# Batch 0's output projection, normalisation and router logits moved into the last attention unit, its shared feed-forward moved ahead of batch 1's projection

## The chip, the cores and the metric

One core of one Trainium2 chip runs the whole layer in one launch. The metric is the device time of that launch in microseconds (us); for the kernel before it is 554.7 us, the median of three runs (551.94, 554.70 and 554.82).

## What is computed

Two post-normalised blocks on 2048 tokens (B = 2 batches of T = 1024) of width 256, all in float32:

```python
x = _layernorm(x + attn(x, Wq, Wk, Wv, Wo))   # 16 heads of 16, 4 key/value heads, ALiBi, causal softmax
...
logits = x @ router_w.T                       # 8 experts, the best one per token
scores = sigmoid(top_vals)                    # of the chosen expert alone
routed = (up * silu(gate)) @ down_proj[e]     # on x * score, by expert
shared = silu(x @ shared_gate_w) * (x @ shared_up_w) @ shared_down_w
x = _layernorm(x + shared + routed)
```

The norms have no weights. The shared feed-forward (hidden width 512) is done for every token; the routed one for the one expert of each token.

## The kernel before, in words

Each engine has its own program, written out by hand, and the engines meet at semaphores only. An engine runs its program strictly in the order of the code, so a wait holds up all that stands behind it. The same is true of SP, which issues nearly all DMAs, and of POOL, which issues the rest.

**Attention.** The work is cut into NU = 8 units, one for each batch and key/value head (four query heads); units 0 to 3 are batch 0, units 4 to 7 are batch 1. A unit is 9 groups of four tiles. A tile is one score matmul of 128 keys by 512 queries (`score`, L528, matmul at L537), one exp on ACT into `probs` (`weights`, L802, at L807) and two 32-column float32 matmuls with the values (`weigh`, L540, at L548). Scores go through SB = 3 PSUM banks (4, 5, 6), so the score of tile i waits for the exp of tile i - 3. POOL zeroes half of the diagonal tiles (L1155). `step(u)` on PE (L564) walks the nine groups by the strings in `ORDER`: S is a score, W the weighing of the group before, M a row-maximum tile of the next units (`max_tile`, L506), which DVE reduces (L879). In the last unit no M is left: its groups hold SSSWS alone. The maxima of unit 7 are taken during unit 6; DVE then turns them (L913 to L930) and SP writes them back (`max_rows`, L317). ACT copies the two banks of outputs and denominators to SBUF, one in the middle of the unit and one after its end (L816, L821), and SP stores them to DRAM as `yT` (`store_y`, L311).

**Between attention and experts.** For each batch SP loads the denominators from DRAM (`load_den`, L327), DVE inverts them (`invert`, L943), SP stores the result and waits until it is there (`store_rden`, L332), and loads it in another layout (`load_rden`, L346); the unnormalised outputs come with 8 DMAs per chunk of 512 tokens (`load_yT`, L338). For batch 0 all this happens while unit 7 runs (L433 to L438), for batch 1 after it (L440 to L450). There are NCH = 4 chunks, 0 and 1 of batch 0. PE does for each chunk c `spread(c)` (L605, one reciprocal to all rows, two instructions of 512 columns), `project(c)` (L612, four token tiles, two matmuls, so four instructions of 256 columns, each, in banks 2 and 3 by turns) and `route(c)` (L624: eight transposes, a copy of them by ACT at L830, and 16 logit instructions of 8 columns). DVE does `normalise(c)` (L949), `residual(c)` (L954: an add, a bn_stats and a bn_aggr for each tile) and `scale_rows(c)` (L965), with the inverse root on POOL between them (L1173). The order on PE is L672 to L703, on DVE L971 to L982. After the fourth chunk one pass chooses the expert of all 2048 tokens (L996 to L1008), PE ranks the tokens (L694 to L701), and DVE works out each token's slot (L1023 to L1045).

**Shared feed-forward.** `gate_up(n)` (L642) for n = 0 to 15: chunk n // 4, hidden block n % 4, eight instructions of 512 columns; it waits for `hidden(n - 2)`. ACT does Silu (L837), DVE the product (`hidden`, L1010). `down(c)` (L652) is 32 instructions of 256 columns; DVE adds the result into `x_all` (L1056). That add also waits until POOL has scaled the tile's rows by the score (L1189), since it overwrites them. POOL then scatters the rows by expert with 16 indirect DMAs (L1193). PE's order is `gate_up(0)`, `route(3)`, `gate_up(1)`, the ranking, then L702 to L715.

**Experts.** 23 tiles of 128 rows (L756 to L762). The change only swaps the PSUM banks of their gate and up products.

Where the buffers lie: `x1T` (the turned, normalised tokens) is in `probs`, which the last unit is using until its end; `hT` and `sG` of the shared feed-forward are in `tmp`, beside `yTc`, `rdc` and `den`.

Of the kernel before, what the change touches and what calls it, by code (L numbers as in the profile page):

```python
# [11 lines left out]
P = 128  # L12
# [88 lines left out]
ORDER = (SHORT, LONG) * 4 + (SHORT,)  # L101
assert NA % 2 == 0 and GROUPS % STEP == 0 and sum(o.count("M") for o in ORDER) == NA

# [18 lines left out]
def layer(nc, x_d, xT_d, wq_d, wk_d, wv_d, wo_d, rt_d, gu_d, dn_d, sg_d, su_d, sd_d, cf_d, cb_d, al_d, one_d, zero_d, thq_d, thk_d,  # L122
          out_d):
    with ExitStack() as ctx:
# [33 lines left out]
        x1T = pr2[:, 0:KC * NTOK].rearrange("p (k t) -> p k t", k=KC)  # L158
# [22 lines left out]
        hT = tmp[:, 0:2048].rearrange("p (f t) -> p f t", f=FC)  # L181
        hT0 = tmp[:, 3072:3584]
        sG = [tmp[:, 2048 + i * 512:2048 + (i + 1) * 512] for i in range(2)]
# [42 lines left out]
        def hidden_part(c, f):  # L226

            return hT0 if f == 0 and c % 2 else hT[:, f, :]

# [54 lines left out]
        def _(sp):  # L284
# [194 lines left out]
        def _(pe):  # L479
# [121 lines left out]
            for u in range(NU):  # L601
                step(u)


            def spread(c):  # L605

                pe.wait_ge(s_ch[c], 16 * (KC * TPC + 1))
                if c >= 2:
                    pe.wait_ge(s_yn, c - 1)
                pe.matmul(ps[:, c % 2, :], sel, rdc[c % 2], start=True, stop=True).then_inc(s_rb, 1)  # L610

            def project(c):  # L612
                pe.wait_ge(s_yn, c + 1)
                for t in range(TPC):
                    n = c * TPC + t
                    at = TPC - 1 - t if c % 2 else t
                    if n >= 2:
                        pe.wait_ge(s_res, n - 1)
                    for kc in range(KC):
                        mm = pe.matmul(ps[:, 2 + n % 2, 0:C], yTc[c % 3][:, kc, at * P:(at + 1) * P], wo[:, kc, :],  # L620
                                       start=kc == 0, stop=kc == KC - 1)
                    mm.then_inc(s_op, 1)

            def route(c):  # L624
# [3 lines left out]
                for kc in range(KC):  # L628
                    for t in range(TPC):
                        mm = pe.transpose(ps[:, 4 + kc, t * P:(t + 1) * P],  # L630
                                          x_all[:, c * TPC + t, kc * P:(kc + 1) * P], idf)
                    mm.then_inc(s_tp, 1)
                pe.wait_ge(s_x1T, KC * (c + 1))
                for t in range(TPC):
                    n = c * TPC + t
                    for kc in range(KC):
                        mm = pe.matmul(ps[:, 6, n * E:(n + 1) * E], x1T[:, kc, n * P:(n + 1) * P], rt[:, kc, :],  # L637
                                       start=kc == 0, stop=kc == KC - 1)
                mm.then_inc(s_lg, 1)


            def gate_up(n):  # L642
                c, f = n // FC, n % FC
                if n >= 2:
                    pe.wait_ge(s_h, n - 1)
                for w, bank, done in ((wsg, 0, s_g), (wsu, 1, s_u)):
                    for kc in range(KC):
                        mm = pe.matmul(ps[:, bank + 2 * (n % 2), :], w[:, kc, f * P:(f + 1) * P],  # L648
                                       x1T[:, kc, c * CH:(c + 1) * CH], start=kc == 0, stop=kc == KC - 1)
                    mm.then_inc(done, 1)  # L650

            def down(c):  # L652
                pe.wait_ge(s_h, FC * (c + 1))
                for t in range(TPC):
                    n = c * TPC + t
                    if n >= 2:
                        pe.wait_ge(s_acc, n - 1)
                    for f in range(FC):
                        mm = pe.matmul(ps[:, 4 + n % 2, 0:H], hidden_part(c, f)[:, t * P:(t + 1) * P], wsd[:, f, :],  # L659
# [12 lines left out]
            pe.wait_ge(s_wo, 32)  # L672
            pe.wait_ge(s_yev, 2 * NU + 2)
            spread(0)
            for c in range(NCH):
                if c % 2 == 0:
                    spread(c + 1)
                project(c)
                if c >= 1:
                    route(c - 1)  # L680
# [605 lines left out]
```

## Time and profile before

| what | us |
|---|---|
| median of three runs | 554.70 |
| the profiled execution's own time | 557.83 |
| its span, first to last instruction | 556.1 |
| PE busy in the span | 514.5 (93%) |
| DVE busy | 298.9 (54%) |
| ACT busy | 229.1 (41%) |
| POOL busy | 177.5 (32%) |
| mean granted TensorE clock, as a share of 2.4 GHz | 0.972 |

The profile is of one execution. PE, DVE, ACT and POOL are the compute engines, PEld is PE's weight load, which runs beside its matmuls, SP issues DMAs (SPq is its queue). "Busy" is time in which an instruction is under way; the granted clock says at which of TensorE's two speeds (1.0 is 2.4 GHz, 0.50 is 1.2 GHz). Matmuls overlap, so the spacing of their starts, and not the duration of one, says what a row of them costs. L with a number is a line of the kernel before. PE's share of the chain that ended last is 81%.

### The profile page before, as it was taken

Reading aid. Unit: us, or ns where it says so; the run is one execution under the profiler, and the core shown is the slowest. Engines: PE = TensorE matmul, PEld = TensorE weight load, DVE = VectorE, ACT = ScalarE, POOL = GpSimd, SP = SyncE. Lnnn points to the kernel's source line nnn. Section 1 sums busy time; section 2 is a strip of 40 time slices with the busy share of each in tenths; the row PEclk is TensorE's granted clock in tenths of the full one; section 3 lists DMA queues with packets and bytes.
Section 4 is the critical chain, followed back from the end, with each engine's and each line's share of the span. In section 5 each row is a group of like instructions: output and inputs, shape, how many; then the busy total and the mean of one; then the engine's idle time right before and its main releaser. Section 6 shows DMA issues by size and latency. Waiting matters only on the chain.

```text
span 556.1 us, 7466 instructions
## 1 busy us (share of the span) xinstructions
PE 514.5 (93%) x2538; PEld 256.4 (46%) x2538; DVE 298.9 (54%) x624; ACT 229.1 (41%) x465; POOL 177.5 (32%) x247
## 2 busy tenths in 40 slices
PE   5987999999999999988889899989999999999991
PEld 2432333333333333321166655555656666566661
DVE  1789888888888888860075451211213333334241
ACT  3441676767676767678601131101112222322220
POOL 4432223322222222222100109730022554545543
PEclk9999999999999999999977989999999999999997
DMA  7772455545453545071328100320121221222210
GB/s 225 134 194 73 78 170 89 159 89 175 86 180 87 179 82 183 20 239 47 101 66 285 44 0 1 132 76 20 57 85 49 66 76 59 68 76 57 66 48 28
DMA packets 36868, 54.92 MB, mean 99 GB/s; under 512 B 5647, under 2 KB 24931, under 8 KB 36724
## 3 DMA queue, kind: packets, MB, share of 16 engines
q1 hardware_dynamic: 29792, 30.96, 21.3%
q0 software_dynamic: 7040, 23.50, 13.5%
q8 instruction: 21, 0.34, 0.3%
q14 instruction: 15, 0.12, 0.1%
HBM read 34.76 MB, written 17.52 MB: 94 GB/s over the span
## 4 chain that ended last, share of the span: by engine, by line
PE 81%; DVE 10%; ACT 4%; issue 2%; DMA 1%; POOL 1%; POOLq 0%; SPq 0%; ACTq 0%; DVEq 0%
PE ps L728 14%; PE ps L548 11%; PE ps L523 10%; PE ps L648 10%; PE ps L537 9%; DVE mx L879 7%; PE ps L747 7%; PE ps L659 5%; PE ps L493 3%; PE ps L620 3%; PE ps L739 2%; ACT probs L807 2%; PE ps L525 2%; PE ps L637 1%; PE ps L610 1%
## 5 line engine op out<-in xcount | busy, mean ns | idle before, releaser
L879 DVE TENSOR_REDUCE mx<-ps 128x1 f32<-128x512 f32 (+4 forms) x312 | 183.0, 643 | 29.0 <-PE ps L525 20.9
L807 ACT ACTIVATE probs<-ps 128x512 f32<-128x512 f32 x288 | 151.1, 606 | 68.6 <-PE ps L537 68.6
L523 PE MATMUL ps<-qk_or_dn 127*128 127x512 bf16 (+3 forms) x384 | 117.4, 331 | 5.5 <-DVE mx L879 3.9
L537 PE MATMUL ps<-qk_or_dn 127*128 127x512 bf16 x288 | 100.5, 380 | 2.9 <-ACT probs L807 2.6
L1155 POOL TENSOR_SCALAR_AFFINE_SELECT probs<-probs 128x512 f32<-128x512 f32 x64 | 40.5, 633 | 164.5 <-ACT probs L807 164.5
L728 PE MATMUL ps<-wgu,tmp 128*128 x184 | 82.9, 593 | 0.1
L548 PE MATMUL ps<-probs,Vs 128*32 128x512 f32 x576 | 76.7, 605 | 0.7 <-ACT probs L807 0.7
L523 PEld LDWEIGHTS ps<-qk_or_dn 127*128 127x128 bf16 x384 | 37.1, 97 | 80.1 <-DVE mx L879 63.7
L1203 POOL DMA_INDIRECT rows<-acc,tok x23 | 22.7, 986 | 89.9 <-DMA acc<-x_all 45.1
L1068 DVE TENSOR_TENSOR tmp<-tmp,ps 128x512 f32<-128x512 f32 x23 | 15.8, 688 | 65.0 <-PE ps L728 65.0
L525 PE MATMUL ps<-cb 128*128 128x128 bf16 x256 | 50.6, 222 | 0.0
L728 PEld LDWEIGHTS ps<-wgu,tmp 128*128 128x128 f32 x184 | 33.3, 190 | 33.3 <-issue 33.3
L537 PEld LDWEIGHTS ps<-qk_or_dn 127*128 127x128 bf16 x288 | 27.1, 98 | 41.7 <-ACT probs L807 23.6
L860 ACT ACTIVATE tmp<-ps 128x512 f32<-128x512 f32 x23 | 13.7, 597 | 74.9 <-PE ps L739 74.9
L747 PE MATMUL ps<-qk_or_dn,tmp 128*128 x184 | 43.6, 380 | 0.8 <-ACT tmp L860 0.8
L747 PEld LDWEIGHTS ps<-qk_or_dn,tmp 128*128 128x128 f32 x184 | 34.9, 190 | 15.1 <-issue 11.5
L837 ACT ACTIVATE tmp<-ps 128x512 f32<-128x512 f32 x16 | 9.4, 597 | 65.2 <-PE ps L648 59.5
L525 PEld LDWEIGHTS ps<-cb 128*128 128x128 bf16 x256 | 25.1, 98 | 14.1 <-issue 1.3
L648 PE MATMUL ps<-probs,wsu 128*128 128x512 f32 x64 | 31.2, 611 | 0.0
L659 PE MATMUL ps<-wsd,tmp 128*128 128x256 f32 x128 | 28.8, 381 | 2.3 <-issue 1.4
L648 PE MATMUL ps<-probs,wsg 128*128 128x512 f32 x64 | 30.9, 606 | 0.0
L493 PE MATMUL ps<-probs,yU 128*128 128x512 f32 x48 | 24.4, 645 | 6.0 <-DMA yU<-in_wq 6.0
(121 smaller groups left out, 470.9 us busy)
## 6 DMA issues: line engine op xcount, KB each, us to landing
wgu<-in_gu POOLq DMA_DIRECT2D x8, 1024.0 KB, 6.1
qk_or_dn<-qparts SPq DMA_DIRECT2D x36, 128.0 KB
yT<-yU SPq DMA_DIRECT2D x16, 256.0 KB, 2.1
qk_or_dn<-in_dn SPq DMA_DIRECT2D x8, 512.0 KB, 8.0
tmp<-xs SPq DMA_DIRECT2D x23, 128.5 KB
qparts<-wgu SPq DMA_DIRECT2D x6, 384.0 KB, 3.3
tmp<-yT SPq DMA_DIRECT2D x34, 64.0 KB
xs<-rows POOLq DMA_DIRECT2D x1, 2056.0 KB, 10.2
```

The costliest lines, as they stand in the source:

```text
L493: mm = pe.matmul(ps[:, 4 + n % 4, :], w, xTc[:, c, kc, :], start=kc == 0, stop=kc == KC - 1)
L523: mm = pe.matmul(o, q, K6[k][0:KROWS, k0:k0 + w], start=True, stop=not masked)
L525: mm = pe.matmul(o[:, diag:diag + P], id16, mask_qk, start=False, stop=True)
L537: pe.matmul(o, K6[k][0:KROWS, kb * P:(kb + 1) * P], Q6[k][0:KROWS, :, qi * P:(qi + 1) * P], start=True, stop=True).then_inc(s_st, 1)
L548: mm = pe.matmul(ps[32 * j:32 * j + VP, 2 + bank, :], Vs[:, u % STEP, kb, :], probs[:, 4 * (s % 3) + p, :], start=begins, stop=ends, skip_ ...
L648: mm = pe.matmul(ps[:, bank + 2 * (n % 2), :], w[:, kc, f * P:(f + 1) * P], x1T[:, kc, c * CH:(c + 1) * CH], start=kc == 0, stop=kc == KC - 1)
L659: mm = pe.matmul(ps[:, 4 + n % 2, 0:H], hidden_part(c, f)[:, t * P:(t + 1) * P], wsd[:, f, :], start=f == 0, stop=f == FC - 1)
L728: mm = pe.matmul(ps[:, 2 * k + half_i, :], xsT[k][:, kc, :], wgu[:, bass.ds(e * (KC * 2 * I) + (kc * 2 * I + half_i * I), I)], start=kc == ...
L747: mm = pe.matmul(ps[:, 7, 0:H], ehT[j % 2][:, f, :], wdn[:, bass.ds(experts[j] * (FC * H) + f * H, H)], start=f == 0, stop=f == FC - 1)
L807: act.activation(probs[:, 4 * (s % 3) + p, :], ps[:, 4 + (4 * s + p) % SB, :], ACT.Exp, scale=SCALE).then_inc(s_exp, 1)
L879: dve.tensor_reduce(o, ps[:, a_bank(u, t), 0:nh * w].rearrange("p (h w) -> p h w", h=nh), AX.X, ALU.max).then_inc(s_amax, 1)
L1155: pool.affine_select(tile, tile, [[0, HG], [1, P]], ALU.is_ge, zero, base=0, channel_multiplier=-1).then_inc(s_mask, 1)
```

## The change

- In the last unit PE follows `LAST_ORDER` in place of `ORDER`: in group 3 both spreads of batch 0 (R), in groups 4 and 5 the eight projections of its tiles (P), in group 7 the transposes of chunk 0 (T), in group 8 its logits (L). DVE, ACT and POOL get the matching work at the matching places of their programs.
- SP loads batch 0's denominators and its 16 pieces of `yT` before its step of unit 6, no longer after it. `store_rden(0)` and the two `load_rden` stay after that step. `invert(0)` moves into DVE's stream of maxima for unit 7, eight tiles from its end.
- `route` is split into `turn` (transposes) and `logits`. After the last unit PE does the four `gate_up` of chunk 0 with chunk 1's transposes and logits between them, then spreads and projects batch 1, then `down(0)`, then chunk 1's `gate_up` with the transposes, logits and ranking of batch 1 between them.
- The choice of the expert is done for each batch by itself (`choose`, `confidence`, `odds`), so ACT's Exp at the old L832 comes twice, between Silus. POOL scales batch 0's rows before it does the inverse roots of chunks 2 and 3.
- `x1T` of batch 0 moves to the part of `qk_or_dn` that no longer holds a unit; the down-projection weights of experts 4 and 5, which go there, are loaded last, after `gate_up(7)`. `hT` and `sG` move to `probs`. PSUM banks are dealt out anew.

```diff
+LAST_ORDER = ("SSSWS", "SSSWS", "SRSSWRS", "SPSPSPWPS", "SPSPSPWPS", "SSSWS", "STSSWS", "SLSSWS", "W")
...
+        x1T = [qk_or_dn[:, 2 * KC * T:3 * KC * T].rearrange("p (k t) -> p k t", k=KC),
+               pr2[:, 0:KC * T].rearrange("p (k t) -> p k t", k=KC)]
...
             for u in range(NU):
+                if u == NU - 2:
+                    load_den(0)
+                    for c in range(2):
+                        load_yT(c)
                 step(u, u % STEP, last=u == NU - 1, more=u + 2 < NU)
                 if u == NU - 2:
-                    load_den(0)
                     store_rden(0)
                     for c in range(2):
-                        load_yT(c)
                         load_rden(c)
...
             for c in range(2, NCH):
-                if c == 3:
-                    sp.wait_ge(s_op, TPC)
-                    load_yT(c)
                 sp.wait_ge(s_rb, c - 1)
                 load_rden(c)
-            for e in range(E):
+                if c == 2:
+                    sp.wait_ge(s_op, TPC)
+                    load_yT(3)
+            for e in (0, 1, 2, 3, 6, 7, 4, 5):
+                if e == 4:
+                    sp.wait_ge(s_u, 2 * FC)
...
             pe.wait_ge(s_wsh, 48)
             gate_up(0)
+            turn(1)
             gate_up(1)
+            logits(1)
             gate_up(2)
             gate_up(3)
-            for c in range(NCH):
+            spread(2)
+            spread(3)
+            for n in range(NT // 2, NT):
+                project(n)
+            down(0)
+            turn(2)
+            gate_up(4)
+            turn(3)
+            gate_up(5)
+            logits(2)
+            logits(3)
+            gate_up(6)
+            rank()
+            gate_up(7)
+            for c in range(1, NCH):
...
                 for s in range(1, GROUPS):
                     weights(u, s)
+                    if last and s == GROUPS - 2:
+                        copy_turned(0)
...
+                if n == 4:
+                    copy_turned(2)
+                if n == 5:
+                    copy_turned(3)
+                act.activation(sG[n % 2], ps[:, gate_bank(n), :], ACT.Silu).then_inc(s_sg, 1)
+                if n == 0:
+                    copy_turned(1)
+                if n in (1, 5):
+                    odds(n // 5)
...
+                        if u == NU - 1 and t == NA - 9:
+                            invert(0)
...
+            normalise(0)
+            normalise(1)
+            residual(0)
+            residual(1)
+            scale_rows(0)
+            scale_rows(1)
+            hidden(0)
+            invert(1)
+            hidden(1)
+            choose(0)
+            confidence(0)
+            hidden(2)
+            hidden(3)
+            normalise(2)
+            normalise(3)
+            residual(2)
+            residual(3)
+            scale_rows(2)
+            scale_rows(3)
+            accumulate(0)
+            hidden(4)
+            hidden(5)
+            choose(1)
+            confidence(1)
+            hidden(6)
+            slots()
+            hidden(7)
...
+                    if u == NU - 1 and s in (5, 7):
+                        inverse_root(s // 7, s_bn, 2 * TPC * (s // 7 + 1), s_rstd, s // 7 + 2)
```

The new `project(n)` does one token tile (banks 7 and 0 for batch 0, 0 and 1 for batch 1) and waits for the residual add of tile n - 2; `down(0)` waits for the last residual add; `logits(0)` waits for `copy_turned(0)`, which ACT does after the exps of group 7.

## Rows read from the trace of the kernel before

**Rows 1.** Busy time by stretch, all engines; last columns granted clock, DMA share, GB/s
```profile
254.70:274.80 20.10, 17.80 (x102) 3.81 (x101) 0.95 (x1) 16.94 (x34) 4.44 (x7) 1.00 0.28 88
274.80:328.80 54.00, 47.64 (x216) 33.30 (x217) 29.16 (x80) 7.63 (x13) 5.09 (x8) 0.81 0.33 107
328.80:408.60 79.80, 76.94 (x251) 45.93 (x248) 19.14 (x45) 9.31 (x18) 30.18 (x33) 1.00 0.15 50
```

**Rows 2.** Timeline of the last attention unit, PE and ACT: one group
```profile
267.81 0.82 PE L537 MATMUL ps<-qk_or_dn 127*128 127x512 bf16 x3
268.24 2.06 ACT L807 ACTIVATE probs<-ps 128x512 f32<-128x512 f32 x4 [0.33 <-PE ps L537]
...
268.89 0.39 PE L537 MATMUL ps<-qk_or_dn 127*128 127x512 bf16 x1 [0.26 <-ACT probs L807]
...
270.21 0.82 PE L537 MATMUL ps<-qk_or_dn 127*128 127x512 bf16 x3
```

**Rows 3.** Chain of work that ended last, between attention and experts
```profile
305.47 1.09 ACT probs L830 x2
...
306.61 1.95 PE ps L637 x16
308.56 3.56 PE ps L620 x16
...
328.95 13.84 PE ps L648 x32
342.79 6.91 PE ps L659 x32
```

**Rows 4.** Busy time of PE by stretch, with the granted clock
```profile
286.30:289.70 3.40, 0.78 (x4) 1.00 0.16 47
289.70:293.10 3.40, 3.40 (x13) 0.51 0.34 100
293.10:296.50 3.40, 2.71 (x20) 0.99 0.59 186
296.50:303.40 6.90, 6.90 (x14) 0.51 1.02 339
```

**Rows 5.** Timeline of SP's queue: unit 6's last store, then batch 1's loads
```profile
254.93 0.33 SPq L314 DMA_DIRECT2D yT<-yU  x1
...
279.59 0.60 SPq L328 DMA_DIRECT2D tmp<-yT  x1
...
280.24 5.01 SPq L342 DMA_DIRECT2D tmp<-yT  x8
...
286.51 0.32 SPq L334 DMA_DIRECT2D rden<-tmp  x1
...
288.05 0.33 SPq L347 DMA_DIRECT2D tmp<-rden  x1
...
293.39 0.46 SPq L347 DMA_DIRECT2D tmp<-rden  x1
```

**Rows 6.** Timeline of the other engines: what one instruction of each kind takes
```profile
257.85 0.95 DVE L945 RECIPROCAL tmp<-tmp 128x128 f32<-128x128 f32 x1 [11.28 <-DMA tmp<-yT]
...
296.72 0.28 PEld L610 LDWEIGHTS ps<-tmp,cf 16*128 16x128 f32 x1 [0.40 <-DMA tmp<-rden]
...
297.65 1.22 DVE L951 TENSOR_TENSOR tmp<-tmp,ps 128x1024 f32<-128x1024 f32 x1 [4.51 <-PE ps L610]
...
310.02 0.43 DVE L960 BATCH_NORM_STATS2 bst<-x_all 128x6 f32<-128x256 f32 x1
...
314.79 1.38 DVE L967 TENSOR_SCALAR x_all<-x_all,mv,rstd 128x256 f32<-128x256 f32 x4 [1.47 <-POOL rstd L1178]
...
323.70 1.28 ACT L837 ACT_TABLE_LOAD   x1
...
333.33 11.73 POOL L1189 TENSOR_SCALAR rows<-x_all,score 128x256 f32<-128x256 f32 x13
...
367.13 0.96 POOL L1193 DMA_INDIRECT xs<-rows,slot  x1 [0.30 <-issue]
```

More of the change, by code:

```diff
@@ L808, in weights, with copy_turned @@
                                    ).then_inc(s_exp, 1)
+            def copy_turned(c):
+                for kc in range(KC):
+                    act.wait_ge(s_tp, KC * c + kc + 1)
+                    act.activation(x1T_part(c)[:, kc, :], ps[:, turn_bank[c][kc], :], ACT.Copy).then_inc(s_x1T, 1)
             def step(u, last=False):
@@ L825, in _, with odds @@
                 step(u, last=u == NU - 1)
-            for c in range(NCH):
-                for kc in range(KC):
-                    act.wait_ge(s_tp, KC * c + kc + 1)
-                    act.activation(x1T[:, kc, c * CH:(c + 1) * CH], ps[:, 4 + kc, :], ACT.Copy).then_inc(s_x1T, 1)
-            act.wait_ge(s_rt, 2)
-            act.activation(score[:], top[:], ACT.Exp, scale=-1.0).then_inc(s_ez, 1)
+            def odds(b):
+                v = slice(b * NT // 2, (b + 1) * NT // 2)
+                act.wait_ge(s_rt, ROUTE_OPS * b + 2)
+                act.activation(score[:, v], top[:, v], ACT.Exp, scale=-1.0).then_inc(s_ez, 1)
             for n in range(NCH * FC):
@@ L852, in silu @@
                     act.wait_ge(s_eh, j - 1)
-                act.activation(esG[k], ps[:, 2 * k, :], ACT.Silu).then_inc(s_es, 1)
+                act.activation(esG[k], ps[:, 2 * (1 - k), :], ACT.Silu).then_inc(s_es, 1)
             def hidden_T(j):
@@ L968, in scale_rows @@
                                             ALU.subtract, ALU.mult)
[L969 to L982 removed]
+                ins.then_inc(s_x1, 1)
             count = [0]
@@ L1010, in hidden, with confidence @@
+            def confidence(b):
+                v = slice(b * NT // 2, (b + 1) * NT // 2)
+                dve.wait_ge(s_ez, b + 1)
+                chain(dve.tensor_scalar(score[:, v], score[:, v], 1.0, None, ALU.add))
+                dve.reciprocal(score[:, v], score[:, v]).then_inc(s_score, 1)
             def hidden(n):
@@ L1034, in _ @@
-            chain(dve.tensor_tensor(place[:], ps[:, 7, 0:NT * E].rearrange("p (n e) -> p n e", e=E),
-                                    start[:, :].rearrange("p (o e) -> p o e", o=1).broadcast_to([P, NT, E]), ALU.add))
-            chain(dve.tensor_tensor(place[:], place[:], oh[:], ALU.mult))
-            chain(dve.tensor_reduce(slotf[:], place[:], AX.X, ALU.add))
-            chain(dve.tensor_copy(slot[:], slotf[:]))
-            chain(dve.tensor_tensor(after[:], cf[:, CF_J:CF_J + MT].rearrange("p (j o) -> p j o", o=1)
-                                    .broadcast_to([P, MT, E]),
-                                    end[:, :].rearrange("p (o e) -> p o e", o=1).broadcast_to([P, MT, E]), ALU.is_ge))
@@ L1043, in _ @@
-            chain(dve.tensor_reduce(etf[:], after[:], AX.X, ALU.add))
-            chain(dve.tensor_scalar(etf[:], etf[:], float(E - 1), None, ALU.min))
-            dve.tensor_copy(et[:], etf[:]).then_inc(s_slot, 1)
-            for n in range(2, FC):
-                hidden(n)
-            for c in range(NCH):
-                if c + 1 < NCH:
-                    hidden(FC * (c + 1))
+                dve.tensor_tensor(hidden_part(c, f), sG[n % 2], ps[:, gate_bank(n) + 1, :], ALU.mult).then_inc(s_h, 1)
@@ L1062, in hidden_rows @@
+            accumulate(0)
[6 more added lines that the diff above has]
+            hidden(7)
+            for c in range(1, NCH):
+                if c + 1 < NCH:
+                    hidden(FC * (c + 1))
+                accumulate(c)
+                if c + 1 < NCH:
+                    for f in range(1, FC):
+                        hidden(FC * (c + 1) + f)
             def hidden_rows(j):
@@ L1156, in mask_probs, with inverse_root @@
                                    ).then_inc(s_mask, 1)
+            def inverse_root(c, done, value, out_sem, n_out):
+                v = slice(c * TPC, (c + 1) * TPC)
+                pool.wait_ge(done, value)
+                pool.tensor_scalar(rstd[:, v], mv[:, v, 1], EPS, None, ALU.add).then_inc(s_half, 1)
+                pool.wait_ge(s_half, n_out)
+                pool.tensor_tensor(rstd[:, v], rstd[:, v], half[:, v], ALU.pow).then_inc(out_sem, 1)
             for u in range(NU):
```

255 lines of the change are left out of this document (139 added, 116 removed).

## The prediction, made before the changed kernel ran

> **What bounds the kernel now.** I read the busy time by stretch first [rows 1]. In the last unit (254.7 to 274.8) PE is busy for 17.8 of 20.1 us, but its matmuls overlap, and the timeline of one group shows that it waits: a group starts every 2.40 us (267.81, 270.21), three scores go at once, the fourth at 268.89 waits for the first exp, and with the weighing behind it takes the 1.32 us to the next group [rows 2]. At a spacing of 0.22 us (three in 0.82, each 0.38 long) four scores are 0.9 us and the eight weighing instructions 1.0, so some 0.5 to 0.6 us of each group is free on PE. DVE has nothing to do there (0.95 us busy). From 274.8 to 328.8 the picture turns: 54.0 us, ACT and POOL nearly idle, and TensorE's granted clock is 0.81 on average [rows 1]. The two speeds are 1.0 and 0.5, so 38% of the stretch, 20.5 us, ran at 1.2 GHz and cost about 10 us. From 328.8 to 408.6 PE works without a break but for 2.9 us.
>
> The clock's falls are in [rows 4]: after a stretch with 0.78 us of matmuls in 3.4 it stood at 0.51 for 3.4 us; after one with a wait and 16 logits of 8 columns (2.71 us "busy") it stood there for 6.9.
>
> **Full-speed work behind the last unit.** From [rows 3]: four `gate_up` in 13.84 us, 3.44 to 3.46 each, so 55.0 for 16; `down` 6.91, so 27.6 for four; projections of four tiles 3.56, so 0.89 a tile and 14.2 for 16; 16 logits 1.9, so 7.6. A 512-column float32 instruction costs 0.43 (3.44 / 8); a spread has two, 0.86, 3.4 for four; eight transposes of 128 columns at a quarter of 0.43 are an estimated 0.9, 3.6 for four. Ranking and the first two expert-row transposes I estimate at 2.6; that term is the same on both sides. Sum 114.0. The stretch was 133.8 (54.0 + 79.8), so 19.8 us are lost: 10 to the clock, 2.9 in the second part, some 7 to waits for DVE, POOL, ACT and DMAs in the first.
>
> **The last unit after the change.**
> 1. *Spreads and projections.* Between the end of the second weighing and that of the sixth, four groups or 9.6 us before, PE now does in series 16 scores (3.5), four weighings (4.0), two spreads (1.7) and eight projections (7.1): 16.3, and 0.4 of waiting in group 6, so 16.7. Only 2.5 us are absorbed: +7.1. DVE keeps up: a projection comes every 1.1 us (a score and 0.89), and add and statistics take about 0.43 each [rows 6].
> 2. *Transposes of chunk 0.* 0.9 us against 0.5 free: +0.4. Their input is ready about when they come up: last projection, add, statistics, aggregate and 1.38 for scaling [rows 6], some 2.8 us in all, against a group of 2.4.
> 3. *Logits of chunk 0.* They wait on PE for two copies that ACT does after the exps of group 7 (1.09 [rows 3]), and three scores, two weighings and the last exps stand behind them. From the last score of group 7: exp begins at 0.43 [rows 2], copies end at 2.1, logits end at 4.0, two scores and the weighing 5.4, the last score 5.6, its exp done 6.7, last weighing 7.7. Before, that path was 4.6: +3.1.
> 4. *Reciprocals of batch 0.* SP loads denominators and `yT` early, but the store, 1.54 us to its landing (286.51 to 288.05), and the load back stay behind unit 6's last store. From that store (254.93 [rows 5]) they need some 0.4 for the issue, 1.5 and a load of about 2, so they end near 259; the first spread comes up at 258.6, four groups of 2.40 before 268.24: +0.5, between 0 and 2.
> 5. *The inversion within the maxima of unit 7.* 0.95 us on DVE [rows 6], at a place where DVE sets the pace: +0.7, between 0 and 0.95. The unused part of DVE would hide it; PE's maximum tiles wait for it otherwise.
> 6. *Clock.* The logits and the 1.5 us of waiting before them look like the stretches of [rows 4]. A fall of 3.4 us costs 1.7, partly beyond the unit's end where it is covered (below): +1.0, between 0 and 3.4.
>
> Sum 12.8: the unit ends at 287.6 in place of 274.8.
>
> **Behind it.** Work is 114.0 - 11.6 (two spreads, eight projections, one set of transposes, one of logits) = 102.4. Waits are counted from the unit's end.
> - The DMA chain of batch 1 keeps its form [rows 5]: `load_den` at +4.8 (279.59), eight `yT` pieces to +10.4, store of the inverses, load at +12.0, eight more pieces of 5.0 in all, and the last `load_rden` at +17.4. It lands 3.3 later (293.39 to 296.7 [rows 5, 6]): +20.7. PE does four `gate_up`, one set of transposes and of logits, one spread before that: 17.5. So the gate work covers what had been PE's wait, but `spread(3)` still waits 3.2 us.
> - Projections then run at DVE's pace (0.9 a tile after a 1.22 normalise): +1.1. `down(0)` uses the banks of the projections and its third tile waits until DVE has scaled chunks 2 and 3 and added the first tile: +0.6. POOL's 16 row scalings, 0.9 each (11.73 / 13), are cut in two: batch 0's eight end at about +20, so the inverse roots queued behind them, due at +28, are not held up.
> - ACT's extra Exp costs table loads, 1.28 each [rows 6], four more. `odds(0)` stands before Silu 2, which `gate_up(4)` needs 20 us later; `odds(1)` before Silu 6, about 2.5 us late, still ahead of `slots` and of `gate_up(8)`. I cost them at nothing; if slots and ranking ran late, each load would cost up to 1.28. The Trainium skill, ScalarE: Activation LUTs, section What ACT_TABLE_LOAD costs, counts a drain of about 1.38 us to each load, 2.66 in all. The trace shows the load of 1.28 and the Silu at its end, and no run here shows the drain. By that rule Silu 6 and `slots` move back by some 3 us, `gate_up(9)` waits 0.7, and the sum would be 0.7 worse.
> - The splitting of choice and slots costs DVE more small instructions, all beside `gate_up`. The expert stage starts earlier, and its inputs are there: POOL's scatter, 16 DMAs at 1.26 each, issued its last at 367.13 [rows 6], 40 before the experts; now it starts some 60 after the unit's end and takes 20, and the experts come at 111.
> - *Clock.* The 3.2 us wait resembles the first row of [rows 4], and two sets of logits in a row the third: I take a fall behind each, 2.3 us lost on projections and 1.7 on `gate_up(6)`: +4, between 0 and 8.
>
> Sum: 102.4 + 3.2 + 1.1 + 0.6 + 4.0 = 111.3, and the shared part ends at 287.6 + 111.3 = 398.9, where it had ended at 408.6: -9.7. The profiled execution took 557.8 (span 556.1), so its like would be 548.1; the median of the runs is 3.1 below that execution, and against it the time is 554.7 - 9.7 = 545.0.
>
> **Rivals.**
> - *The clock stays up and the small delays don't come.* Without terms 4 to 6 and the 4.0 behind, the gain is 9.7 + 2.2 + 4.0 = 16, some 539. For it: PE gets far fewer bare waits. Against it: both waits of [rows 4] were followed by a fall. Chance 0.15.
> - *Moved, not hidden.* PE becomes the bound of the last unit, and a late input holds it once more: the spread waits 2 us for the reciprocals, the transposes or the logits' copies come late by 1 or 2, and each pause brings a clock fall within the scores. With the upper ends of terms 4 and 6 (+1.5, +2.4) and 2 us on items 2 and 3, the gain is 9.7 - 5.9 = 4, some 551. For it: the unit's scores, spreads and logits are in one queue, and each wait stops all. Chance 0.15, a third of which is within 0.5%.
> - *Slower: TensorE at 1.2 GHz through batch 1's projection.* Place: from `spread(3)` to the end of `down(0)`. PE would wait for reciprocals, then for adds, then for the scaled rows, about 16 us of which 15 are work; at half speed these cost 15 more, not 2.3, and the kernel ends at 545 + 13 = 558. It decides from a low clock of some 28 us in all behind the unit (9.7 more than the 4.0 costed, at half). Against it: no fall in [rows 4] lasted over 6.9. Chance 0.07.
> - *Early loads do not come early.* SP's 17 DMAs, at some 0.6 us each, could delay `max_rows(7)`, and with it the whole unit. They take some 10.5 us, and unit 5's last store lies about a unit, over 20 us, ahead of unit 6's at 254.93 [rows 5], the maxima less than 9 ahead of it, so there seems to be room. The cost would be 1 to 3 us; chance 0.03, time 547.
>
> **How the numbers follow.** The forecast has 0.60. A measurement of this kernel tells some 0.5% (2.8 us) from no change, so faster means under 551.9: the forecast, the first rival, the last and two thirds of "moved" give 0.88, of which I take 0.02 for a tail of the forecast; so faster 0.86, within 0.5% 0.07 (that tail and the third of "moved"), slower 0.07. The range leaves out two tenths: down to 538 (the first rival), up to 551 (the second).
>
> **What would show it.** Right: the last unit's groups 4 and 5 take 5.4 us each instead of 2.4, ACT idle there behind PE; the last weighing is 12 to 13 us later; the wait of PE before logits 0 is about 1.5; a DMA wait of 2 to 4 us at `spread(3)` and no other over 1.5 behind the unit; the shared part 109 to 114 us long; an unchanged expert stage of 147. Wrong: a unit longer by over 15; a mean clock under 0.85 between the unit and `down(1)`; PE waiting for POOL's row scalings or for Silu 6; or an expert stage that waits for its rows.

## The result and the profile after

The changed kernel takes 547.16 us, the median of four runs (543.33 to 548.91), against 554.76 for the kernel before: a ratio of 0.9868, 95% interval 0.983 to 0.9907, or 5.2 to 9.4 us faster. Run again with more repetitions beside the kernel before, it took 548.88 against 554.42, 0.9907 (0.9888 to 0.9926). So the gain is 5 to 8 us, around 1%. The prediction said 545.0, range 538 to 551. Every ratio in this document leaves out executions in a slower state: here none, further down one of `plain` (1318 us), one of `zero_inv` (566 us) and one of the kernel before (1958 us).

The profiled execution seems to say more than that, and the reader should be warned: it took 543.33 us, span 541.6, which is 14.5 less than the span before. It is the fastest of all runs of this kernel. What it lacks is falls of TensorE's granted clock.

Busy time by stretch in the changed kernel, whose lines L have numbers of their own: the last unit, the part to `down(0)`, the part to `gate_up(6)`, the rest up to the experts. The columns are those of [rows 1].

```profile
255.80:289.20 33.40, 30.74 (x163) 13.16 (x162) 12.83 (x34) 18.68 (x36) 7.15 (x12) 0.95 0.06 20
289.20:317.10 27.90, 26.02 (x96) 14.94 (x92) 14.17 (x36) 8.13 (x11) 8.53 (x10) 1.00 0.52 165
317.10:336.70 19.60, 19.31 (x96) 14.23 (x96) 6.20 (x19) 4.43 (x7) 1.34 (x2) 1.00 0.02 5
336.70:394.10 57.40, 56.83 (x214) 34.90 (x214) 17.42 (x45) 8.41 (x16) 22.86 (x24) 1.00 0.26 87
```

The stretch of 54.0 us with a clock of 0.81 in [rows 1] is gone; behind the unit PE is busy for 102.2 of 104.9 us at full clock. The unit itself has grown from 20 to 33.4 us. Its timeline, one line for each weighing, shows where (start and duration; lines between are left out):

```profile
258.29 1.06 PE L568 MATMUL ps<-probs,Vs 128*32 128x512 f32 x8
...
259.96 1.12 PE L626 MATMUL ps<-tmp,cf 16*128 16x512 f32 x2
...
261.55 1.06 PE L568 MATMUL ps<-probs,Vs 128*32 128x512 f32 x8
...
267.17 1.06 PE L568 MATMUL ps<-probs,Vs 128*32 128x512 f32 x8
...
272.69 1.07 PE L568 MATMUL ps<-probs,Vs 128*32 128x512 f32 x8
...
276.04 1.06 PE L568 MATMUL ps<-probs,Vs 128*32 128x512 f32 x8
...
277.71 1.09 PE L649 MATMUL ps<-cf,x_all 128*128 128x128 f32 x8
...
279.16 1.07 PE L568 MATMUL ps<-probs,Vs 128*32 128x512 f32 x8
...
281.08 1.08 ACT L869 ACTIVATE qk_or_dn<-ps 128x512 f32<-128x512 f32 x2
...
282.21 2.18 PE L658 MATMUL ps<-rt,qk_or_dn 128*128 128x8 f32 x16 [1.45 <-ACT qk_or_dn L869]
...
285.19 1.94 PE L568 MATMUL ps<-probs,Vs 128*32 128x512 f32 x8
...
288.18 1.06 PE L568 MATMUL ps<-probs,Vs 128*32 128x512 f32 x8 [0.69 <-ACT probs L863]
```

The weighings came every 2.4 us [rows 2]. Now the two that have four projections ahead of them are 5.6 and 5.5 us behind the one before, and from 258.29 to 276.04 it takes 17.75 in place of 9.6: +8.1. The group with the transposes takes 3.12, +0.7. From 279.16 to the last weighing it is 9.02 us. In it PE waits 1.45 us for ACT's two copies, does the logits, and then the clock is down: eight weighing instructions that take 1.07 elsewhere take 1.94 at 285.19.

Behind the unit, SP's queue and what PE waits for:

```profile
293.16 4.95 SPq L358 DMA_DIRECT2D tmp<-yT  x8
...
294.98 0.95 DVE L1006 RECIPROCAL tmp<-tmp 128x128 f32<-128x128 f32 x1 [1.30 <-DMA tmp<-yT]
...
298.16 0.46 SPq L350 DMA_DIRECT2D rden<-tmp  x1
...
300.74 0.32 SPq L363 DMA_DIRECT2D tmp<-rden  x1
301.11 4.92 SPq L358 DMA_DIRECT2D tmp<-yT  x8
...
306.07 0.46 SPq L363 DMA_DIRECT2D tmp<-rden  x1
...
308.24 1.12 PE L626 MATMUL ps<-tmp,cf 16*128 16x512 f32 x2 [1.34 <-DMA tmp<-rden]
```

Four `gate_up` fill the time in which the DMAs run; the last load is issued 16.8 us behind the unit's end and PE's wait for it is 1.34 us. The inverses were there at 295.93 and lay for 2.2 us, because SP was still issuing pieces of `yT`.

ACT's Exp that was added, at the first of its two places. It needs two table loads, one to Exp and one back to Silu; the second is shown:

```profile
299.42 0.21 ACT L894 ACTIVATE score<-top 128x8 f32<-128x8 f32 x1 [2.01 <-DVE top L1063]
...
299.75 1.28 ACT L904 ACT_TABLE_LOAD   x1
...
301.05 0.60 ACT L904 ACTIVATE probs<-ps 128x512 f32<-128x512 f32 x1
```

The load to Exp was done ahead of Exp's wait (it began at 296.13, Exp at 299.42), and no PE instruction waited for either. The Silu starts 1.42 us behind the end of Exp, so the drain of 1.38 us that the Trainium skill adds to each load (ScalarE: Activation LUTs, What ACT_TABLE_LOAD costs) does not appear beside the 1.28; here the measurement decides.

### The profile page after: what moved, and what is told of

Read it like the earlier page. It is cut to its first block, busy times and chain, and to the rows that moved or that the text cites. A ratio compares the mean times of both kernels' runs of the same rounds, so it can differ in the third digit from the quotient of the medians.

```text
span 541.6 us, 7482 instructions
## 1 busy us (share of the span) xinstructions
PE 505.7 (93%) x2538; PEld 250.7 (46%) x2538; DVE 300.9 (56%) x633; ACT 235.0 (43%) x470; POOL 177.9 (33%) x247
## 4 chain that ended last, share of the span: by engine, by line
PE 76%; DVE 12%; DMA 3%; SPq 2%; ACT 2%; issue 1%; POOL 1%; POOLq 0%; DVEq 0%; ACTq 0%
PE ps L784 15%; PE ps L568 11%; PE ps L543 10%; PE ps L557 8%; DVE mx L950 8%; PE ps L700 8%; PE ps L803 7%; PE ps L713 5%; PE ps L513 3%; PE ps L795 2%; PE ps L545 2%; SPq L358 2%; PE ps L638 1%; PE ps L658 1%; PE ps L723 1%
## 5 line engine op out<-in xcount | busy, mean ns | idle before, releaser
L863 ACT ACTIVATE probs<-ps 128x512 f32<-128x512 f32 x288 | 152.1, 603 | 80.8 <-PE ps L557 80.7
L784 PEld LDWEIGHTS ps<-wgu,tmp 128*128 128x128 f32 x184 | 33.2, 190 | 33.4 <-issue 33.3
L931 ACT ACTIVATE tmp<-ps 128x512 f32<-128x512 f32 x23 | 13.7, 597 | 74.9 <-PE ps L795 74.9
L557 PEld LDWEIGHTS ps<-qk_or_dn 127*128 127x128 bf16 x288 | 27.3, 99 | 37.7 <-ACT probs L863 16.8
L803 PEld LDWEIGHTS ps<-qk_or_dn,tmp 128*128 128x128 f32 x184 | 34.9, 190 | 15.1 <-issue 11.5
L1085 DVE TENSOR_TENSOR probs<-probs,ps 128x512 f32<-128x512 f32 x16 | 11.0, 686 | 40.5 <-PE ps L700 35.6
L713 PE MATMUL ps<-wsd,probs 128*128 128x256 f32 x128 | 28.6, 380 | 0.8 <-DVE x_all L1030 0.6
L904 ACT ACTIVATE probs<-ps 128x512 f32<-128x512 f32 x16 | 9.6, 598 | 43.8 <-PE ps L700 43.8
L1280 POOL TENSOR_SCALAR rows<-x_all,score 128x256 f32<-128x256 f32 x16 | 14.5, 930 | 40.1 <-DVE score L1075 40.1
## 6 DMA issues: line engine op xcount, KB each, us to landing
xs<-rows POOLq DMA_DIRECT2D x1, 2056.0 KB, 11.6
```

The lines of the kernel that those rows point to most:

```text
L557: pe.matmul(o, K6[k][0:KROWS, kb * P:(kb + 1) * P], Q6[k][0:KROWS, :, qi * P:(qi + 1) * P], start=True, stop=True).then_inc(s_st, 1)
L713: mm = pe.matmul(ps[:, n % 2, 0:H], hidden_part(c, f)[:, t * P:(t + 1) * P], wsd[:, f, :], start=f == 0, stop=f == FC - 1)
L784: mm = pe.matmul(ps[:, 2 * (1 - k) + half_i, :], xsT[k][:, kc, :], wgu[:, bass.ds(e * (KC * 2 * I) + (kc * 2 * I + half_i * I), I)], start ...
L803: mm = pe.matmul(ps[:, 7, 0:H], ehT[j % 2][:, f, :], wdn[:, bass.ds(experts[j] * (FC * H) + f * H, H)], start=f == 0, stop=f == FC - 1)
L863: act.activation(probs[:, 4 * (s % 3) + p, :], ps[:, 4 + (4 * s + p) % SB, :], ACT.Exp, scale=SCALE).then_inc(s_exp, 1)
```

## The experiments

The theory: three things happened. The cover behind the unit is the large gain; the unit pays for it nearly in full, since PE does everything in series; and the clock's falls make executions of one kernel differ by several microseconds. The rivals stand with each run, in what was expected of it. The runs were made in three sets, each with the kernel before beside it.

**The changed kernel again, and the kernel before again.** No edit.

> The changed kernel once more, word for word. Theory (schedule plus clock): everything but TensorE's granted clock repeats, so a second profile differs from the first (span 541.6, clock 0.986) by half the difference in time spent at 1.2 GHz; with one to three more falls of 3.4 us the span is 543 to 547, and the median of the runs 1.0% to 1.7% below the kernel before. Rival (the 14.5 us between the two spans is the real gain and the other runs were disturbed by something else): span within 1 us of 541.6 in every profile, median 2.5% below the kernel before.

> The kernel before once more, for a second profile. Theory (the clock's falls vary from execution to execution): the falls between 274 and 330 are at other places or of another number than in the first profile (20.5 us at 1.2 GHz), the span 550 to 556 and equal to 556.1 less half the difference in low-clock time. Rival (the falls belong to the schedule alone): the same four falls, span within 0.5 us of 556.1.

Measured: spans of 544.2 and 553.1 us. I cut each execution in four: from ACT's first copy of unit 6 to the first weighing of unit 7, the unit (to its last weighing's end), from there to the experts' first matmul, and the experts. Times are from the timelines; a fall is given by the time at 1.2 GHz that the granted clock of half-microsecond stretches adds up to.

```
kernel      to unit 7   unit 7   to experts   experts   falls between 250 and 400
before          14.86    19.96       133.93    147.49   6.8, 3.4, 6.8, 3.4 us
before again    14.86    19.95       129.63    147.47   6.8, 10.2
changed         15.38    33.34       104.95    147.47   3.4
changed again   16.40    31.79       108.52    147.41   6.8
```

The experts take the same within 0.1 us in all four. The falls come at other places each time, though the two executions of a kernel have their instructions in the same order: in the first profile of the changed kernel the fall is inside the unit (284 to 287), in the second behind `spread(3)`'s wait (307 to 314), where the eight projections with the 32 instructions take 9.20 us:

```profile
308.02 2.07 PE L626 MATMUL ps<-tmp,cf 16*128 16x512 f32 x2 [2.04 <-DMA tmp<-rden]
310.02 9.20 PE L638 MATMUL ps<-wo,tmp 128*128 128x256 f32 x32
```

The first profile has 7.28 for the same 32. Over ten runs of the changed kernel (four in the result, six here) and the 17 of the kernel before that ran beside the six, the span less what the clock took ((1 - clock) x span) is 533.3 against 537.3 on average, and what the clock took 12.7 (7.6 to 15.9) against 15.3 (12.7 to 16.6). So about 4.0 us of the gain are the schedule's and 2.6 the clock's (3.9 and 2.0 with the six alone). The split is rough: a low clock costs nothing while PE waits, so this figure is the most that the clock can have taken. A single profile can be more than 4 us from the mean (541.6 against 546.0). The rival that 14.5 us were real is out. The median is 0.93% below the kernel before, a little less than the 1.0% to 1.7% expected. Half the difference in low-clock time does not explain the second profiles to the end, though: it leaves 0.9 us in the changed kernel, which is in the stretch before unit 7 (below), and 1.8 in the kernel before, where a pause of 2.3 us on PE in the first profile is missing:

```profile
368.30 1.99 PE L659 MATMUL ps<-wsd,tmp 128*128 128x256 f32 x8 [1.41 <-issue]
...
371.17 1.99 PE L659 MATMUL ps<-wsd,tmp 128*128 128x256 f32 x8 [0.88 <-DVE x_all L1056]
```

**Without the placement in the unit** (`plain`):

```diff
-LAST_ORDER = ("SSSWS", "SSSWS", "SRSSWRS", "SPSPSPWPS", "SPSPSPWPS", "SSSWS", "STSSWS", "SLSSWS", "W")
+LAST_ORDER = ("SSSWS",) * 8 + ("WRRPPPPPPPPTL",)
...
-                    if last and s == GROUPS - 2:
-                        copy_turned(0)
...
+            copy_turned(0)
             for n in range(NCH * FC):
...
-                    if u == NU - 1 and s in (5, 7):
-                        inverse_root(s // 7, s_bn, 2 * TPC * (s // 7 + 1), s_rstd, s // 7 + 2)
...
+            for c in range(2):
+                inverse_root(c, s_bn, 2 * TPC * (c + 1), s_rstd, c + 2)
             pool.wait_ge(s_zf, 48)
```

> Batch 0's spreads, projections, transposes and logits taken out of the last unit and done right behind it, ahead of gate_up(0); all else as changed. Theory (the unit absorbs little PE time, but hides the waits for DVE, POOL and ACT between these steps): the unit ends 13 to 14 us earlier (near 276), then 11.6 us of work with 4 to 6 us of waits and a clock fall or two (2 to 3 us), so 3 to 7 us slower than the changed kernel, 0.6% to 1.3%, and about as fast as the kernel before or up to 0.8% faster. Rival (placing them in the unit gains nothing, since PE does them in series there too): within 0.3% of the changed kernel.

Measured: 550.98 us, 0.9948 (0.993 to 0.9967) of the kernel before, 2.1 us slower than the changed kernel beside it (1.8 us without the execution of 1318 us). The unit is 19.95 us again, the part behind it 124.75. PE waits there for what the unit had hidden:

```profile
277.81 7.28 PE L638 MATMUL ps<-wo,tmp 128*128 128x256 f32 x32 [0.53 <-DVE tmp L1021]
...
287.61 1.09 PE L649 MATMUL ps<-cf,x_all 128*128 128x128 f32 x8 [2.52 <-DVE x_all L1040]
...
289.44 3.47 PE L658 MATMUL ps<-rt,qk_or_dn 128*128 128x8 f32 x16 [0.74 <-ACT qk_or_dn L869]
292.77 3.76 PE L700 MATMUL ps<-qk_or_dn,wsg 128*128 128x512 f32 x4
```

0.5 us for the normalise, 2.5 for scaling, 0.7 for the copy, and a fall that doubles the logits and half a `gate_up` (3.47 in place of 1.85, 3.76 in place of 1.96). The direction of the theory holds, its size does not: placing the steps in the unit gains 1.8 to 2.1 us by the medians and 2.8 by the mean spans, where 3 to 7 were expected, for 11.6 us of PE work moved there. Less the clock's part the spans differ by 3.4 (536.9 against 533.4); the clock took 12.7 here and 13.3 there. That there is no gain at all is out, since the two intervals do not overlap; a gain as small as the 0.3% that the rival allowed is not out.

**Without the cover behind the unit** (`oldtail`):

```diff
-            gate_up(0)
             turn(1)
-            gate_up(1)
             logits(1)
-            gate_up(2)
-            gate_up(3)
             spread(2)
             spread(3)
             for n in range(NT // 2, NT):
                 project(n)
+            for n in range(4):
+                gate_up(n)
             down(0)
```

ACT's and DVE's programs follow that order.

> In-unit work kept as changed; the cover behind the unit taken away: gate_up(0) to gate_up(3) go behind batch 1's projection, so that PE has only chunk 1's transposes and logits while batch 1's denominators and outputs are loaded. Theory (the gate work under the DMA chain is the larger part of the gain): PE idles some 14 us ahead of the spreads, so 12 to 17 us slower than the changed kernel, with a clock fall; that is 0.8% to 1.5% slower than the kernel before. Rival (the chain of DMAs was not what PE waited for): under 5 us slower than the changed kernel.

Measured: 563.95 us, 1.0194 (1.0172 to 1.0216), 15.1 us slower than the changed kernel and 1.9% slower than the kernel before. The 15.1 lies within the 12 to 17 expected; against the kernel before it is slower than the 0.8% to 1.5% expected. The two waits for DMAs are 6.57 and 3.69 us, and their sum of 10.3 is lower than the 14 expected. The changed kernel has 1.3 to 2.0 there, so 8 to 9 us are waits. The clock took up to 23.6 us against 13.3 in the mean of the runs; part of that fell into the waits and cost nothing, and what is left of the 15.1 is of its size. PE timeline and one long stretch with its granted clock:

```profile
304.40 2.07 PE L626 MATMUL ps<-tmp,cf 16*128 16x512 f32 x2 [6.57 <-DMA tmp<-rden]
310.17 2.07 PE L626 MATMUL ps<-tmp,cf 16*128 16x512 f32 x2 [3.69 <-DMA tmp<-rden]
312.16 8.67 PE L638 MATMUL ps<-wo,tmp 128*128 128x256 f32 x32
```

```profile
284.50:315.00 30.50, 18.86 (x60) 10.08 (x61) 5.75 (x14) 4.97 (x8) 7.24 (x8) 0.50 0.32 101
```

So a low clock of 30.5 us does occur, with in-unit work and no cover; in it PE is busy for 18.9 us. It begins at the logits of the unit and stays through both waits. That is the mechanism of the rival "slower", which the changed kernel escaped because `gate_up` stands where this one waits.

**One term at a time.** Three edits to the changed kernel, and all three:

```diff
 invert
-                        if u == NU - 1 and t == NA - 9:
-                            invert(0)
+            invert(0)
 logits
-... "STSSWS", "SLSSWS", "W")
+... "STSSWS", "SSSWS", "W")
             gate_up(0)
+            logits(0)
             turn(1)
 sp
             load_den(1)
-            load_yT(2)
-            store_rden(1)
+            load_half_yT(2, 0)
+            sp.wait_ge(s_rd, 2)
+            sp.dma_start(rden_d[1].rearrange("a j h t -> (a j h) t"), den[:, P:2 * P]).then_inc(s_rds, 16)
+            load_half_yT(2, 1)
+            sp.wait_ge(s_rds, 32)
             for c in range(2, NCH):
                 sp.wait_ge(s_rb, c - 1)
                 load_rden(c)
                 if c == 2:
                     sp.wait_ge(s_op, TPC)
-                    load_yT(3)
+            load_yT(3)
```

> The changed kernel with invert(0) behind DVE's maxima of unit 7 in place of within them. Theory (DVE sets the pace there, so its 0.95 us goes straight into the start of the last unit): the maxima end 1.0 us earlier (near 246.6), unit 7's first scores no longer wait for the written-back maxima, the unit starts and ends 1.0 to 1.2 us earlier, 0.2% faster. Rival (DVE's idle time beside the maxima hides it): no difference in the unit's start.

> The changed kernel with chunk 0's logits behind gate_up(0) in place of within group 8 of the last unit. Theory (on PE they wait 1.5 us for ACT's copies, and scores, exps and the last weighings stand behind them): the unit ends 3.0 us earlier (near 286.2 at full clock, 4 us where the clock fell there), and 1.9 us come back behind it, so 1.0 to 2.5 us faster. Rival (their wait is only moved): within 0.5 us of the changed kernel.

> The changed kernel with SP's order after the last unit altered: the inverses of batch 1 are stored after the first four pieces of yT of chunk 2, and both loads of them are issued ahead of chunk 3's pieces of yT. Theory (spread(3) waits 1.3 to 2.2 us because the last load stands behind 16 pieces of 0.61 us and a store): the last piece lands 1.5 to 2.5 us earlier, PE's wait goes to under 0.5 us, 1.5 to 2.2 us faster, more where the wait made the clock fall. Rival (projection is paced by DVE and the down-projection by its scaling, so the wait only moves there): under 0.7 us.

> The three edits of invert, logits and sp together. Theory (they are terms of one series on PE and add up): 3.5 to 5.5 us faster than the changed kernel, so 1.6% to 2% faster than the kernel before. Rival (the falls of the clock, which come at other places, give back what is won): within 1.5 us of the changed kernel.

```
kernel     median   of before (interval)        to unit 7   unit 7   to experts
invert     548.10   0.9884 (0.9846 to 0.9921)       15.67    35.30       108.16
logits     544.12   0.9804 (0.9776 to 0.9832)       16.22    29.56       108.95
sp         547.66   0.9891 (0.9858 to 0.9925)       15.39    33.73       104.77
best       544.99   0.9831 (0.9797 to 0.9864)       16.17    29.41       107.29
```

The changed kernel did not run in this set, so it is compared by its ratios, 0.9868 and 0.9907. `logits` is the term that counts: the unit is 2.2 to 3.8 us shorter, and the kernel is 3 to 5 us faster than the changed one by the medians, more than was expected, so as a statement on the time the rival (within 0.5 us) is out. But most of the gain is the clock: in its five runs the clock took 8.9 us (5.9 to 10.9) in place of 12.7, and the span less the clock's part is 532.8 in place of 533.3. So on PE the logits' wait and work were mostly only moved, as the rival said; what the time gained is that TensorE ran less at 1.2 GHz. `sp` did in the profile what it was for (both spreads in one row of four, no DMA wait; `invert`, without that edit, shows no such wait either), but its time can't be told from the changed kernel's, and the expected 1.5 to 2.2 us are not shown. `best` is 1.7% faster than the kernel before, as expected, but not faster than `logits` alone: the terms don't add up beyond what a measurement tells.

`invert` went wrong, and usefully so. DVE's maxima did end where they had ended before (6.50 us behind ACT's first copy of unit 6, as before; 6.93 in the changed kernel), yet the unit started no earlier: 15.67. (That its unit is the longest, 35.30, is a fall from 282.5 to 293.) This row, from the waits of PE between 246 and 258, says why:

```profile
PE ps L557 <- DMA qk_or_dn<-mrow: 1.0, 1, 1.0
```

The scores of unit 7 wait for the DMA that brings the maxima back. Neither profile of the kernel before has such a row. In the changed kernel's own two profiles it is 0.3 and 1.3 us, which is most of what sets 15.38 and 16.40 apart, in `logits` 1.2 and in `best` 1.6. What fills the DMA engines is seen by stretch; first the kernel before, then the changed one (clock, DMA share, GB/s):

```profile
244.00:246.00 2.00, 1.00 0.97 316
246.00:248.00 2.00, 1.00 0.60 197
248.00:250.00 2.00, 1.00 0.04 8
```

```profile
244.00:246.00 2.00, 1.00 1.06 275
246.00:248.00 2.00, 1.00 1.01 239
248.00:250.00 2.00, 1.00 0.69 196
250.00:252.00 2.00, 1.00 0.28 92
```

POOL writes 3.0 MB of zeros at this time (issued at 235.1 in the kernel before, 235.8 in the changed one). The 16 pieces of `yT` of batch 0, which the change put there too, seem to stretch the full load by some 4 us, past the maxima's DMAs (issued from 247.64 on).

**The zeroing moved away**, alone, with `invert`, and with all edits:

```diff
-                    if s == 3 and u == NU - 2:
+                    if s == 2 and u == NU - 1:
                         zero_slots()
```

> The changed kernel with POOL's zeroing of the scatter target (2.9 MB of writes) in unit 7 in place of unit 6; nothing else moves. Theory (batch 0's 16 early pieces of yT, put into unit 6, run beside these writes, so the DMA engines are full until 251.5 and the written-back maxima land late): from ACT's first output copy of unit 6 to the first weighing of unit 7 it takes 14.9 us as before, or 15.4 with what the inversion adds, in place of 15.4 to 16.4; PE's wait for the maxima's DMA is gone; 0.5 to 1 us faster. Rival (the inversion on DVE alone delays the unit): that stretch keeps its 15.4 to 16.4 us, and only an earlier inversion helps.

> The zeroing in unit 7 and invert(0) behind the maxima, both. Theory (two causes in a row, the second covers up the first when one alone is taken away): the stretch from ACT's first output copy of unit 6 to the first weighing of unit 7 is 14.9 us again, as in the kernel before; 1.0 to 1.5 us faster than the changed kernel. Rival (one cause): the same as one of the two edits alone.

> All four edits: invert, logits, sp and the zeroing in unit 7. Theory (the wait for the maxima is 1.3 to 1.6 us in the runs of invert, logits and best, and goes): 1.0 to 1.6 us faster than the three edits together, 2.0% to 2.4% faster than the kernel before, near 543. Rival (the clock's falls take it back): as the three edits, 545.

`best3` also has the projections dealt out two to a group, and chunk 0's transposes later (`gate_up(0)` then waits for their copy):

```diff
+LAST_ORDER = ("SSSWS", "SSSWS", "SRSSWRS", "SPSPSWS", "SPSPSWS", "SPSPSWS", "SPSPSWS", "SSSWTS", "W")
...
-                    if last and s == GROUPS - 2:
+                    if last and s == GROUPS - 1:
                         copy_turned(0)
```

> All four edits, and the eight projections dealt out two to a group over groups 4 to 7 in place of four to a group over two, the transposes of chunk 0 in group 8. Theory (each group has some 0.5 us free on PE, and four groups absorb twice what two do): each of the four groups takes 3.7 us, 5.1 us more in all against 6.3 measured, so about 1.2 us faster than the four edits. Rival (what is absorbed is lost at the unit's end, where transposes and their copies come too late for gate_up(0)): equal or slower.

```
kernel     median   of before (interval)        to unit 7   unit 7   to experts
zero       551.32   0.9895 (0.9848 to 0.9943)       15.31    31.76       114.01
zero_inv   553.02   0.9911 (0.9880 to 0.9941)       14.88    33.44       116.22
best2      546.82   0.9791 (0.9758 to 0.9824)       14.87    29.34       113.53
best3      548.21   0.9833 (0.9798 to 0.9869)       14.87    28.03       112.32
```

In this set, which ran on another chip than the two before it, the kernel before took 557.57 us, so only the ratios compare with the others. The question of the unit's start is settled: 15.31 without the zeroing and with no DMA wait of PE (the 0.45 that is left is the inversion), 14.88 without both, as in the kernel before. There are two causes, and the second hid the removal of the first. In time, `zero` and `zero_inv` gained nothing that can be measured, so their expected 0.5 to 1.5 us is not shown. `best2` has the lowest ratio, 0.9791, within the 2.0% to 2.4% expected, but its interval overlaps that of `logits`.

`best3` shortened the unit as expected (28.03 against 29.34; its four groups take 3.7 us each), but the time did not follow: 0.9833. The runs on record say where it went: the mean span less the clock's part is 1.1 us shorter than that of `best2` (535.3 against 536.4), as expected, and the clock took 10.7 us (7.1 to 12.1) in place of 8.2 (6.5 to 9.3). Why it fell more is open.

All four have a part behind the unit 5 to 9 us longer than their like in the sets before. That must not be put down to the zeroing: less the clock's part, the kernel before, which has no such edit, is 3.1 us longer in this set too (540.4 against 537.3), and it was not profiled in it. A share is on DVE while POOL issues its scatter; this is `zero`, DVE's timeline:

```profile
363.15 0.68 DVE L1085 TENSOR_TENSOR probs<-probs,ps 128x512 f32<-128x512 f32 x1
369.92 0.69 DVE L1085 TENSOR_TENSOR probs<-probs,ps 128x512 f32<-128x512 f32 x1 [6.09 <-issue]
```

DVE stands 6.09 us with nothing to wait for that the profile shows, and PE then waits 3.08 for it. All four profiles of this set have such pauses, which cost PE 3.7 to 4.5 us each time, with DVE coming back 3 to 4 us behind the last of the 16 scatter issues. Of the other profiles only the first of the kernel before has such a pause, the 2.3 us shown above. Whether the set or the edit makes it, and what it is, stays open; nothing was run on it.

## Why the prediction was right, and which terms were off

Point by point, with the profile of the changed kernel and, where given, the second one:

- *Spreads and projections, +7.1, and the reciprocals, +0.5.* Together 7.6 predicted, 8.1 measured. PE in series was right. The two spreads take 1.05 us each and not 0.86, the projections 7.3 in all and not 7.1. The weight load of the first spread waited 0.56 for its data, which put PE's own start off by some 0.2. The prediction's "2.5 us are absorbed" does not follow from its own terms: 8.8 us of work for +7.1 are 1.7, and measured are 0.7.
- *Transposes, +0.4.* Measured +0.7 in both profiles (3.12 and 3.13 for the group).
- *Logits and their copies, +3.1, and the clock, +1.0.* Measured 9.02 for a path of 4.5, so +4.5 with the fall. The second profile has no fall there and takes 7.45, so +3.0; the 1.45 us wait is in both and is the 1.5 predicted:

```profile
279.82 1.06 PE L568 MATMUL ps<-probs,Vs 128*32 128x512 f32 x8
...
285.20 1.07 PE L568 MATMUL ps<-probs,Vs 128*32 128x512 f32 x8
...
287.27 1.06 PE L568 MATMUL ps<-probs,Vs 128*32 128x512 f32 x8 [0.69 <-ACT probs L863]
```

- *Inversion, +0.7.* The stretch grew by 0.52 and, again, 1.54. DVE's part is 0.45. The rest, 0.1 and 1.1, is a collision of DMAs, which the prediction had as a rival ("early loads do not come early", 0.03) but with the wrong mechanism: SP still issued the maxima's DMAs in time (247.64, as DVE ended at 247.61), though its 16 pieces took 13.1 us to issue beside the zeroing and 9.9 without it; it was the DMA engines that had no room.
- *The chain of batch 1.* Last load at +16.8 (predicted 17.4), PE's wait 1.3 and 2.0 (predicted 3.2): in both profiles `spread(3)` starts 2.2 us behind the load's issue, not 3.3. Why the load landed sooner is not shown.
- *Projections of batch 1, +1.1, and `down(0)`, +0.6.* The 32 instructions take 7.28 for 7.1 of work, and `down(0)` waits 0.61 and 0.22: +1.0 in place of +1.7.
- *POOL, slots, table loads, the expert stage.* Costed at nothing; no wait of PE for any of them, and 147.5 us of experts in all.
- *The clock behind the unit, and in the sum.* This is the term that was mis-sized. I had 5 us lost to it after (1.0 and 4.0), against 10.3 before. By the runs, falls took up to 12.7 us of the span after and 15.3 before, of which some 6 lie outside the changed stretch (in the first profile 7.6 were lost in all, and the one fall in it cost 1.7); so in the stretch it is nearer 7 than 5. The gain from the clock was 2.6 us and not 5.3.
- *The schedule's part.* 9.7 less 5.3 is 4.4 us, and 4.0 were measured. Part of that agreement is luck. Less the clock's part, what lies behind the unit was predicted at 107.3 us and took 105.0 and 105.1, but the unit and the stretch before it grew by 12.2 and 13.4 in place of 11.8; and the sum was made against an execution that, less the clock's part, was 3.2 us longer than the mean of the kernel before (540.5 against 537.3).
- *The baseline.* The first profile of the kernel before held a pause of 2.3 us on PE that was counted as lost for good and is not in the second profile, and that execution was the slowest of its set. A sum made against one execution carries that.
- *Signs named beforehand.* Met: groups of 5.5 to 5.6 us, a wait of 1.45 before the logits, an expert stage of 147. Missed: the last weighing came 13.6 to 14.5 us later and not 12 to 13, the wait at `spread(3)` was 1.3 in one of two profiles and not 2 to 4, and the shared part was 105.0 and 108.5 us long, below the 109 to 114 named.

So the gain was 9.7 predicted and 5 to 8 measured, on the right side and inside the range. Of the rivals, the mechanism of "slower" was seen in `oldtail` alone; "moved, not hidden" describes the PE work well: without a fall the unit grew by 11.8 us (31.79 less 19.96) for 11.6 us moved into it. What was gained came from waits that are gone and from a clock that fell less.

## What to carry to other kernels

Work put into a stretch whose engine is in order costs nearly its full length there if the slack is in pieces shorter than the work (0.7 of 8.8 us were absorbed with the projections four to a group; `best3`, with two to a group, absorbed 0.5 a group); what it can hide is the latency of other engines, and a step that itself waits (here the logits on two copies) belongs elsewhere. Fill the time of a DMA chain with dense work that is already due, since here that removed the wait and most of the low clock behind it. Before moving loads earlier, look at who uses the DMA engines then, and not only at the queue that issues them; and take a second profile, and split the mean spans into schedule and clock, before believing a difference of a few microseconds.

## What was not expected of the hardware

- With no instruction reordered, the time that TensorE spent at 1.2 GHz between 250 and 400 us differed between executions: 20.5 and 17 us in the kernel before, 3.4 and 6.8 in the changed one.
- In `oldtail` the granted clock stood at 0.50 for 30.5 us, in which PE was busy for 18.9 us and waited 6.6 and 3.7 us for DMAs.
- Three sets of runs, on three chips, gave the kernel before 554.4, 554.2 and 557.6 us: comparisons across sets need the ratio.
